# GRU with a depthwise convolution on one core: x loads spread out, tap tiles of 96 columns, two orders changed at ScalarE, and thirteen steps' output stores issued by GpSimd

## What is computed

```
x = x + causal_depthwise_conv(x, cond) + b
h = cond
for t in 0..63:
    gi = x[:, t] @ W_ih + b_ih ; gh = h @ W_hh + b_hh
    r = sigmoid(gi_r + gh_r) ; z = sigmoid(gi_z + gh_z) ; n = tanh(gi_n + r * gh_n)
    h = (1 - z) * n + z * h
    out[:, t] = x[:, t] + h
```

## Time and profile before

| | us |
|---|---|
| runs | 1217.53, 1217.55, 1219.98 (median 1217.55) |
| the profiled execution: its time | 1216.99 |
| its span, first to last instruction | 1215.2 |
| TensorE busy | 1155.8 (95%) |
| VectorE, ScalarE, GpSimd busy | 691.6, 508.2, 113.2 |
| steps 1 to 13, with the bulk | from 79.5 to 393.3 of the span |

### The profile page before, as it was taken

One profiled execution on the slowest core, in us unless ns is written; L12 is line 12 of the kernel. 1 busy time (PEld: TensorE's weight loads), 2 busy tenths in 40 slices (PEclk: granted clock), 3 DMA queues, 4 the chain that ended last, 5 costly groups with the idle time before them and its releaser, 6 DMA issues.

```text
span 1215.2 us, 16681 instructions
## 1 busy us (share of the span) xinstructions
PE 1155.8 (95%) x5796; PEld 974.9 (80%) x5796; DVE 691.6 (57%) x1026; ACT 508.2 (42%) x965; POOL 113.2 (9%) x123
## 2 busy tenths in 40 slices
PE   1997999898989989999999999999999999999997
PEld 1985888787868868888888888888888888888885
DVE  2735666565656446555555555555556565555554
ACT  4435777576756333233333333333333322333332
POOL 0400000000000151000111111111111110011110
PEclk9998999899999989999999999999999999999999
DMA  9977888788853701111001111110111111110100
GB/s 254 296 175 145 177 174 181 175 183 167 168 152 95 171 21 35 35 36 33 27 27 35 35 35 35 35 29 27 30 35 35 35 35 35 35 30 27 31 26 26
DMA packets 290088, 101.20 MB, mean 83 GB/s; under 512 B 212944, under 2 KB 282576, under 8 KB 288000
## 3 DMA queue, kind: packets, MB, share of 16 engines
q1 hardware_dynamic: 285696, 99.44, 34.8%
q10 hardware_dynamic: 4352, 1.25, 0.4%
HBM read 66.49 MB, written 34.14 MB: 83 GB/s over the span
## 4 chain that ended last, share of the span: by engine, by line
PE 84%; ACT 4%; issue 3%; DMA 3%; SPq 3%; DVE 3%; POOL 1%; ACTq 0%; DVEq 0%
PE bank L1064 33%; PE sum_a L1122 16%; PE sum_c L1122 12%; PE bank L1156 7%; PE bank L1160 3%; PE sum_c L1064 3%; PE sum_a L1086 3%; PE bank L1026 2%; PE sum_a L1053 2%; PE sum_c L1086 2%; DMA w_again<-in_L_cond_W_ih_dram 1%; SPq L420 1%; ACT tmp L701 1%; DVE q L969 1%; PE sum_c L1053 1%
## 5 line engine op out<-in xcount | busy, mean ns | idle before, releaser
L1064 PE MATMUL bank<-w_hh_hi,hT_hi 128*128 128x512 f32 x584 | 230.0, 394 | 5.0 <-DVE hT_lo L823 5.0
L1064 PE MATMUL bank<-w_hh_lo,hT_hi 128*128 128x512 f32 x584 | 229.1, 392 | 0.0
L1064 PE MATMUL bank<-w_hh_hi,hT_lo 128*128 128x512 f32 x584 | 228.3, 391 | 0.0
L768 ACT ACTIVATE n_gate<-q 128x512 f32<-128x512 f32 x64 | 40.5, 633 | 250.3 <-DVE q L969 250.3
L1064 PEld LDWEIGHTS bank<-w_hh_hi,hT_hi 128*128 128x128 f32 x584 | 110.8, 190 | 27.4 <-DVE hT_lo L823 5.4
L1064 PEld LDWEIGHTS bank<-w_hh_hi,hT_lo 128*128 128x128 f32 x584 | 110.4, 189 | 24.1
L1064 PEld LDWEIGHTS bank<-w_hh_lo,hT_hi 128*128 128x128 f32 x584 | 110.8, 190 | 17.9
L823 DVE TENSOR_TENSOR hT_lo<-bank,hT_hi 128x512 fp32r<-128x512 f32 x64 | 44.2, 690 | 100.5 <-ACT hT_hi L811 100.2
L874 DVE TENSOR_TENSOR x_parts<-x_unit,x_parts 128x512 fp32r<-128x512 f32 x64 | 70.6, 1103 | 44.5 <-ACT x_parts L691 44.4
L811 ACT ACTIVATE hT_hi<-bank 128x512 fp32r<-128x512 f32 x63 | 37.8, 600 | 138.4 <-PE bank L1026 138.4
L757 ACT ACTIVATE r<-bank 128x512 f32<-128x512 f32 x64 | 38.3, 599 | 124.5 <-PE bank L1160 113.1
(11 more groups left out here) (152 smaller groups left out, 2369.1 us busy)
## 6 DMA issues: line engine op xcount, KB each, us to landing
x_unit<-in_x_dram SPq DMA_DIRECT2D x64, 256.0 KB, 4.9
toep_ring<-kernel_parts SPq DMA_DIRECT2D x128, 128.0 KB, 3.4
out_dram<-outZ SPq DMA_DIRECT2D x256, 64.0 KB, 1.6
xres<-stage SPq DMA_DIRECT2D x32, 384.0 KB, 4.7
xT<-xres SPq DMA_DIRECT2D x192, 64.0 KB, 1.9
early<-early_result SPq DMA_DIRECT2D x4, 1024.0 KB, 13.3
xT<-early SPq DMA_DIRECT2D x60, 64.0 KB, 2.0
w_ih_raw<-in_L_cond_W_ih_dram SPq DMA_DIRECT2D x12, 256.0 KB, 7.7
```

Of the source, the lines that this page charges most:

```text
L768: nc.scalar.activation(n_gate[:, :], q[:, :], ACT.Tanh).then_inc(n_ready, 1)
L1064: mm = nc.tensor.matmul(psum[:, :], a[:, rows], b[w][:, cols], start=False, stop=stop and n == 2, skip_group_check=True)
```

## The change

- **x loads.** A unit is loaded in single transfers at pieces 0, 1, 3, 4, 6, 7, 9 and 10 after its first one, over eleven pieces instead of seven. Of unit 1 four transfers go before the bulk instead of eight, the other four at pieces 1, 2, 4 and 5.
- **Tap tiles.** Only the 48 late times (`LATE`) of each half are kept: a tile has 96 columns, so the output has 96 partitions; the transfers bring runs of 48 elements instead of 64. The matmul with the low half of the taps has 128 moving columns (x's high part alone), so the product low*low is left out.
- **Orders at ScalarE.** From step 17 on, the bias of the next step's n gate (`put_bias(ps_hn)`) goes after the copies for the paired products instead of before them. In steps 15 and 16 `hT_hi` goes before `combo_high`.
- **Output stores.** Those of steps 0 to 12 are issued by GpSimd, on semaphores of their own; SyncE no longer waits for the output in these steps, and loads the x of step t+3 at the middle of step t instead of that of step t+4 at its end.

```
-    TOEP = 2 * BLOCK * P
+    TOEP = 2 * BLOCK * 2 * LATE
...
+            X_PARTS_AT = [3 * part // 2 for part in range(8)]
...
-            for b4 in range(4):
-                load_x_quarter(1, b4)
+            for part in range(4):
+                load_x_part(1, part)
...
-                unit, b4 = (m + 21) // 16, (m + 21) % 16 // 2
-                if m % 2 and 2 <= unit < NUNIT and b4 < 4:
-                    if b4 == 0:
+                unit, at = (m + 5) // 16 + 1, (m + 5) % 16
+                if unit < NUNIT and at in X_PARTS_AT:
+                    if at == 0:
                         sp.wait_ge(x_lo_ready, (unit - 1) * UNIT // BLOCK)
-                    load_x_quarter(unit, b4)
+                    load_x_part(unit, X_PARTS_AT.index(at))
...
                     bulk(t, point)
+                    if isinstance(t, int) and 0 < t <= BULK_LAST and point == POINTS // 2 and t - 1 + RING < EARLY:
+                        sp.wait_ge(outT_ready, t)
+                        load_early_xT(t - 1 + RING)
+                if isinstance(t, int) and t < BULK_LAST:
+                    return
...
+            for t in range(BULK_LAST):
+                pool.wait_ge(outZ_ready, t + 1)
+                for q4 in range(QUADS):
+                    pool.dma_start(
+                        out[:, t:t + 1, :].rearrange("(Q s) o (q e) -> q s Q (o e)", s=QUAD, e=P)[q4],
+                        outZ[t % 2][q4 * QUAD:(q4 + 1) * QUAD, :].rearrange("s (Q e) -> s Q e", e=P),
+                    ).then_inc(early_out_stored[t % 2], 16)
...
-                if not direct(i, u, 1) and not last(i, u):
-                    put_bias(ps_hn, bias_hn[:, :], bias_hn_put)
                 if begins:
                     keep_first(0)
...
+                if not direct(i, u, 1) and not last(i, u):
+                    put_bias(ps_hn, bias_hn[:, :], bias_hn_put)
                 first_half(bulk_bank(t, 3))
...
+                if not last(i, u):
+                    act.wait_ge(hT_done, t + 2)
+                    nc.scalar.activation(hT_hi[:, :], ps_hT[:, :], ACT.Copy).then_inc(hT_hi_ready, 1)
                 if not isinstance(i, bass.RuntimeValue) and EARLY - 1 <= t <= EARLY:
                     for n in range(2):
                         combo_high(2 * (t - EARLY + 1) + n)
-                if not last(i, u):
-                    act.wait_ge(hT_done, t + 2)
-                    nc.scalar.activation(hT_hi[:, :], ps_hT[:, :], ACT.Copy).then_inc(hT_hi_ready, 1)
...
+                elif t >= 2:
+                    dve.wait_ge(early_out_stored[u % 2], 16 * QUADS * (t // 2))
...
-                        at = (slot * 2 + low) * P
-                        mm = nc.tensor.matmul(conv_bank[m % 3][:, pair * 2 * B:(pair + 1) * 2 * B],
-                                              toep[j % T_RING][:, at:at + P],
-                                              parts[j % HL_RING][:, slot * 2 * B:(slot + 1) * 2 * B],
-                                              start=low == 0, stop=low == 1)
+                        at = (slot * 2 + low) * 2 * LATE
+                        late = toep[j % T_RING][:, at:at + 2 * LATE]
+                        cols = B if low else 2 * B
+                        mm = nc.tensor.matmul(conv_bank[m % 3][0:2 * LATE, pair * 2 * B:pair * 2 * B + cols], late,
+                                              parts[j % HL_RING][:, slot * 2 * B:slot * 2 * B + cols],
+                                              start=low == 0, stop=low == 1, skip_group_check=True)
```

More of the change, by code:

```diff
@@ L106, in conv_residual_gru @@
     toep_at = top[0]
-    TOEP = 2 * BLOCK * P
-    toep_ring = place("toep_ring", T_RING * TOEP, F32R)
+    TOEP = 2 * BLOCK * 2 * LATE
+    toep_ring = place("toep_ring", T_RING * 2 * BLOCK * P, F32R)
     toep = [toep_ring[:, n * TOEP:(n + 1) * TOEP] for n in range(T_RING)]
@@ L259, in conv_residual_gru @@
         out_stored = [sem(f"out_stored{n}") for n in range(2)]
+        early_out_stored = [sem(f"early_out_stored{n}") for n in range(2)]
+        POOL_STORES = (BULK_LAST // 2 + 1, BULK_LAST // 2)
         w_again_loaded = sem("w_again_loaded")
@@ L414, in load_xT, with load_x_part @@
                     ).then_inc(xT_loaded[u], 16)
[L416 to L423, removed]
+            def load_x_part(unit, part):
+                b4, c = part // 2, part % 2
+                ch = unit * 2 * UNIT + c * UNIT
+                bs = slice(b4 * B // 4, (b4 + 1) * B // 4)
+                sp.dma_start(
+                    x_unit[unit % 2][c * T:(c + 1) * T, :].rearrange("s (b g) -> s b g", g=UNIT)[:, bs],
+                    x[bs, :, ch:ch + UNIT].rearrange("b s g -> s b g"),
+                ).then_inc(x_unit_loaded[unit % 2], 16)
+            X_PARTS_AT = [3 * part // 2 for part in range(8)]
             def load_toep(j):
@@ L429, in load_toep @@
                     first = kernel_parts[ch:ch + BLOCK, :, 0:T]
-                    source = bass.AP(first.tensor, first.offset, [[1, T], [P, 2 * BLOCK], [1, T]])
+                    source = bass.AP(first.tensor, first.offset, [[1, T], [P, 2 * BLOCK], [1, LATE]])
                     sp.dma_start(
                         toep[j % T_RING][c * T:(c + 1) * T].bitcast(F32).rearrange(
-                            "s (n e) -> s n e", e=P)[:, :, c * T:(c + 1) * T],
+                            "s (n e) -> s n e", e=2 * LATE)[:, :, c * LATE:(c + 1) * LATE],
                         source,
@@ L442, in store_stage @@
                     sp.dma_start(xres[0:LATE, e:e + STAGE, :].rearrange("u g b -> u (g b)"),
-                                 stage[n % 2][c * T:c * T + LATE, :]).then_inc(stage_stored[n % 2], 16)
+                                 stage[n % 2][c * LATE:(c + 1) * LATE, :]).then_inc(stage_stored[n % 2], 16)
             for n in range(QUARTERS):
@@ L450, in _ @@
             sp.wait_ge(k_parts_stored, 16 * QUADS)
-            for b4 in range(4):
-                load_x_quarter(0, b4)
+            for part in range(8):
+                load_x_part(0, part)
             for j in range(T_RING):
@@ L488, in step @@
                 if isinstance(t, int):
-                    if t + RING < EARLY:
-                        load_early_xT(t + RING)
                     if t == BULK_LAST:
@@ L510, in _ @@
             for n in range(2):
-                sp.wait_ge(out_stored[n], 16 * QUADS * T // 2)
+                sp.wait_ge(early_out_stored[n], 16 * QUADS * POOL_STORES[n])
+                sp.wait_ge(out_stored[n], 16 * QUADS * (T // 2 - POOL_STORES[n]))
         @block.gpsimd
@@ L620, in _ @@
                 first = conv_b[c * UNIT:(c + 1) * UNIT]
-                act.dma_start(bias_pair[c * T:(c + 1) * T, :].rearrange("s (n g) -> s n g", g=UNIT),
-                              bass.AP(first.tensor, first.offset, [[0, T], [2 * UNIT, NUNIT], [1, UNIT]])
+                act.dma_start(bias_pair[c * LATE:(c + 1) * LATE, :].rearrange("s (n g) -> s n g", g=UNIT),
+                              bass.AP(first.tensor, first.offset, [[0, LATE], [2 * UNIT, NUNIT], [1, UNIT]])
                               ).then_inc(conv_bias_loaded, 16)
@@ L700, in first_half @@
                 for pair in range(2):
-                    nc.scalar.activation(tmp[m % 2][:, pair * B:(pair + 1) * B],
-                                         conv_bank[m % 3][:, pair * 2 * B:pair * 2 * B + B], ACT.Identity,
-                                         bias=bias_pair[:, 2 * m + pair:2 * m + pair + 1]).then_inc(tmp_ready, 1)
+                    nc.scalar.activation(tmp[m % 2][0:2 * LATE, pair * B:(pair + 1) * B],
+                                         conv_bank[m % 3][0:2 * LATE, pair * 2 * B:pair * 2 * B + B], ACT.Identity,
+                                         bias=bias_pair[0:2 * LATE, 2 * m + pair:2 * m + pair + 1]).then_inc(tmp_ready, 1)
             def combo_high(n):
@@ L885, in second_half @@
                 nc.vector.tensor_tensor(
-                    stage[s % 2][:, at:at + 2 * B].rearrange("p (g b) -> p g b", b=B),
-                    conv_bank[m % 3][:, :].rearrange("p (g l b) -> p g l b", l=2, b=B)[:, :, 1, :],
-                    tmp[m % 2][:, :].rearrange("p (g b) -> p g b", b=B),
+                    stage[s % 2][0:2 * LATE, at:at + 2 * B].rearrange("p (g b) -> p g b", b=B),
+                    conv_bank[m % 3][0:2 * LATE, :].rearrange("p (g l b) -> p g l b", l=2, b=B)[:, :, 1, :],
+                    tmp[m % 2][0:2 * LATE, :].rearrange("p (g b) -> p g b", b=B),
                     ALU.add).then_inc(stage_ready, 1)
```

4 lines of the change are left out of this document (2 added, 2 removed).

## The result

The changed kernel takes 1178.03 us (median of four runs, 1176.76 to 1179.38), the kernel before, run beside it, 1218.38 (1217.53 to 1219.98): a ratio of 0.9667, 95% interval 0.9651 to 0.9684. The forecast was 1178, in a range of 1167 to 1205. The sum was met; what follows shows that its terms were not all met, and that the misses nearly cancelled.

The account below looks back on a forecast made before the run. TensorE, busy 95% of the span, was taken as the bound, standing still where SyncE's in-order issuing had fallen behind. From 1216.99 us, terms -23.6 - 6.8 - 8.6 = -39.0 gave 1178 us, range 1167 to 1205.

Parts of the forecast that it names:

- SyncE's order: Bulk steps: x spread, stores moved away and the GRU's x earlier end four issue stalls and their half-clock stretches; -23.6 us.
- the tally for the first stall: SyncE's queue before tap block 4: four x transfers -6.1 us, one of unit 1 +1.5, store -3.0, GRU's x -1.9.
- 3 us of 26.6: Part of the 26.6 us lost in steps 2, 6, 9 and 11 that the forecast left as not won.
- block 6: Tap block called tightest next: issue at 107.2, landing at 111, wanted at piece 12, about 114; only 3 us in hand.
- Narrower bulk: Bulk pieces: 256 matmuls with 128 moving columns go from 0.1175 to 0.084 us each; -8.6 us.
- Steps 15 and 16: hT_hi ahead of combo_high at ScalarE: 7.8 us lost there, about 1 given back in step 16; -6.8 us.
- The n gate's bias: ScalarE from step 17 on: the later bias has its reader most of a step later, no TensorE wait; 0 us.
- Saturation: Rival: bulk transfers reach their limit, so 10 to 29 us come back with the half clock, say 1197 us; chance 0.12.
- Dear narrow matmuls: Rival: bulk fp32r matmuls with 128 moving columns cost 0.219 us each, more than with 256; 1210 us; chance 0.09.
- GpSimd as the bound: Rival: GpSimd's four stores outlast a step of 21.1 us and VectorE's transpose waits; 1268 us at 7 a store; chance 0.04.

## Why the prediction was right, and where it was not

**SyncE's order, -23.6 forecast, -19.1 in the profiles.** That what SyncE had to issue was the reason, and not the bytes to be moved, is shown: taking the stores off SyncE carries the gain, in both directions, and the bytes of the stores are the same. Three things were wrong. I gave the gain to three edits together and made the tally for the first stall out of x mostly; spread x alone does take that stall away, but nearly as much is lost later, and it brings next to nothing over all. I counted with one price for each issue, and the tap tiles' loads got dearer when the stores were gone. And I left 3 us of 26.6 where about 8 are left in steps 2 to 13. The 3 us were meant for block 6, in step 2, but no wait came there (21.30 us); the five that are left stand in steps 4, 5, 8, 10 and 11. SyncE's queue of the changed kernel, ahead of the wait of step 5:

```profile
169.83 2.17 SPq L446 DMA_DIRECT2D xres<-stage  x2
172.04 0.77 SPq L422 DMA_DIRECT2D x_unit<-in_x_dram  x1
172.85 4.96 SPq L405 DMA_DIRECT2D xT<-early  x4
177.86 1.26 SPq L435 DMA_DIRECT2D toep_ring<-kernel_parts  x2
```

and TensorE there:

```profile
181.64 0.59 PE L1105 MATMUL sum_a<-x_parts,toep_ring 128*96 128x256 f32 x4 [1.74 <-issue]
...
183.19 0.63 PE L1081 MATMUL bank<-w_hh_lo,hT_hi 128*128 128x512 f32 x1
```

Four loads of the GRU's x, which I had at 1.88 us, held SyncE for 4.96. They are not the whole reason: with x bunched they took 3.85 at this place, and TensorE did not wait. TensorE stood for 1.74, and 1.5 us after it went on its matmuls ran at the lower clock (0.63 instead of 0.39; the granted clock of the step is 0.93), so the step lost 3.5. The Trainium skill ("DMA: Bandwidth & Descriptors", Issuing engines are not separate DMA queues) says that issuing from another engine only saves the time of issuing, usually little beside the transfer. The first half agrees with the runs. The second does not hold here: that time was worth 17.3 us by the run with the stores back, and 18.6 in steps 1 to 13 by the run with the stores alone, because tap tiles stood behind it.

**Narrower bulk, -8.6 forecast, -5.9 measured.** The piece now, changed kernel, four matmuls and their follower:

```profile
200.27 0.54 PE L1105 MATMUL sum_c<-x_parts,toep_ring 128*96 128x256 f32 x4
200.66 0.44 PE L1081 MATMUL bank<-w_hh_hi,hT_hi 128*128 128x512 f32 x1
200.94 0.40 PE L1081 MATMUL bank<-w_hh_lo,hT_hi 128*128 128x512 f32 x1
```

0.39 us from the first to the follower, as forecast (0.40), but the follower is held back by 0.28 - 0.23 = 0.05, which I had read for the transposes and then left out for the pieces. From the clean steps, a low matmul costs 0.1175 - 0.46/20 = 0.095 us, not 0.084, and with 128-column weights 0.1175 - 0.17/20 = 0.109, near the transposes' 0.1125. So the width of the weights does count at 128 moving columns, as I had assumed, but a quarter fewer of them gave 13%, not 25%. The Trainium skill ("TensorE: Matmul & The Clock Gate", LDWEIGHTS) has a load of weights take columns/1.2 ns, by estimate 107 for 128 columns and 80 for 96: the first agrees with the 109, the second is not reached (95).

**Steps 15 and 16, -6.8 forecast, -7.4 measured.** ScalarE in steps 16 and 17 of the changed kernel:

```profile
402.65 0.60 ACT L823 ACTIVATE hT_hi<-bank 128x512 fp32r<-128x512 f32 x1 [4.13 <-PE bank L1043]
403.34 1.58 ACT L724 ACTIVATE combo_hi<-combo_raw 128x768 fp32r<-128x768 f32 x2
...
420.41 3.04 ACT L724 ACTIVATE combo_hi<-combo_raw 128x768 fp32r<-128x768 f32 x4
423.35 0.62 ACT L728 ACTIVATE xT_hi<-xT 128x512 fp32r<-128x512 f32 x1
```

`hT_hi` no longer waits for GpSimd, step 16 took 17.26 (forecast 17.3), and 0.4 was given back in step 17 (I had about 1), where the two other combinations now stand ahead of `xT_hi`.

**The n gate's bias, 0 forecast, -5.4 measured.** This is the step that failed: "Its reader is the next step's n product, most of a step later, and TensorE shows no wait there. 0." I looked only for who needs the bias, which gives "no loss"; the gain lies with what stood behind it, the seed of `sum_a`, and what it is worth are the 5.4 us from step 18 on of the run with this edit alone. The list that I read does not show it; that of the weight loads has it with 8.3 us.

So the sum was right by luck, its misses cancelling: in the profiles +4.5 for the stalls and +2.7 for the bulk against -0.6 and -5.4. By the medians the kernel gained 2.7 us more than by the two profiles. The other profiles of the same bulk (9.3 and 12.3 above clean) show that stalls differ by that much from run to run; that they make this difference is likely and not shown.

**The rivals.** Saturation: the share over steps 2 to 12 is 0.84, not over 0.9, and it is hardly higher in the steps with the two longest waits (0.84 and 0.88); it did not come. Dear narrow matmuls: 0.095, not 0.219. GpSimd as the bound: four stores take it 2.2 us of a step of 21.3.

## What to carry to other kernels

Compare the lengths of equal steps and the waits of the weight loads, and not only the list of TensorE's waits: a wait of a few tenths of a microsecond is hidden under a matmul's shown end, and 19 of them made up most of 5.4 us here. When an in-order queue is behind, take away what others don't need from it (here the stores) rather than spread the rest, which here only moved the stall. Ask of an instruction that is moved back not only who needs it, but what stood behind it.

## What was not expected of the hardware

- A store of 64 KB costs GpSimd 0.55 us to issue, between SyncE's median (0.45) and mean (0.65) for the same 52 stores, and lands in 3.0 us (median) against 1.9. Nothing shows that it disturbed VectorE or was held up by it: VectorE's transpose into `outZ` takes 712 ns in the mean in both kernels, and the longest issue is 0.69 us.
- An issue at SyncE has no fixed price: with the stores gone, and nothing else but the place of the GRU's x changed, its tap tiles' loads took 116.9 us together instead of 104.5.
- Two standstills of nearly the same length had different prices. After the one of 1.74 us in step 5 the clock was 0.93 over the step, which lost 3.5; after the one of step 8, 1.9, it stayed at 1.00, and the step lost 2.3. No run here was made to tell why.
- With 256 moving columns the width of the weights (128 or 96) makes no difference to the hundredth (21.77 a step), with 128 moving columns it makes 0.29 us in twenty low matmuls.
